# Two neighbouring nodes in one partition: 512-byte rows of x and of the output, and every second column of adj read by TensorE

## The reference

```
h = relu(layernorm(x)); e = par * (diag * h @ W) + h        # W, par, diag of users / of items
x = x + layernorm(adj @ (adj.T @ e)) * gamma + beta + h     # layer 0: adj and its transpose
h = relu(layernorm(x)); x = x + adj @ h                     # layer 1
h = relu(layernorm(x)); x = x + chebyshev(adj, h) + bias    # layer 2: three products with adj
h = relu(layernorm(x))                                      # layer 3
x = x + relu(d * ((adj + I) @ (d * (h @ W3 + b)))), d = degree ** -0.5
```

## Time and profile before

| | us |
|---|---|
| median of 3 runs | 1507.28 (1506.65 to 1507.91) |
| the profiled execution | 1505.76 |
| its span in the trace | 1503.9 |
| TensorE busy (matmul) in it | 1468.5 (98%) |
| VectorE / ScalarE / GpSimd busy | 377.2 / 256.9 / 84.4 |
| mean DMA rate | 354 GB/s |
| granted TensorE clock, mean | 0.997 of 2.4 GHz |

### The profile page before, as it was taken

How to read it: one execution, slowest core, us unless ns; L and a number is a source line. 1 busy time by engine, 2 the same in 40 slices (tenths; PEclk the granted TensorE clock), 3 DMA queues, 4 the chain that set the end, 5 groups by cost and what they waited for, 6 DMA issues and landing times.

```text
span 1503.9 us, 17963 instructions
## 1 busy us (share of the span) xinstructions
PE 1468.5 (98%) x7901; PEld 628.6 (42%) x7901; DVE 377.2 (25%) x383; ACT 256.9 (17%) x510; POOL 84.4 (6%) x67
## 2 busy tenths in 40 slices
PE   6999999999999998999999999999999999999996
PEld 4555555555555653333333333333333333333331
DVE  5683543443443424110110200000000011110210
ACT  3334334344344352000000000000000000000000
POOL 2300000000000017200000000000000000000000
PEclk9999999999999999999999999999999999999999
DMA  9899999999999999999998777979797845598997
GB/s 325 337 415 414 400 392 389 387 386 399 377 396 361 358 396 423 420 421 421 420 420 316 297 280 294 411 292 356 291 319 269 305 172 226 233 398 336 394 420 303
DMA packets 103217, 532.66 MB, mean 354 GB/s; under 512 B 19388, under 2 KB 19428, under 8 KB 55268
## 3 DMA queue, kind: packets, MB, share of 16 engines
q1 hardware_dynamic: 96052, 529.84, 89.8%
q10 hardware_dynamic: 7088, 1.67, 0.5%
HBM read 425.32 MB, written 106.17 MB: 353 GB/s over the span
## 4 chain that ended last, share of the span: by engine, by line
PE 92%; DMA 6%; DVE 1%; POOL 1%; ACT 0%; issue 0%; ACTq 0%; POOLq 0%; DVEq 0%
PE acc L466 34%; PE turned L466 31%; PE turned L492 12%; PE t_acc L477 12%; DMA over_last<-adj_t 6%; PE t_acc L607 1%; DMA w_in<-in_L_gnn_W_i_dram 0%; PE turned L633 0%; PE turned L639 0%; PE acc L518 0%; PE t_rows L617 0%; PE t_acc L542 0%; POOL rstd L982 0%; PE t_rows L531 0%; ACT staged L677 0%
## 5 line engine op out<-in xcount | busy, mean ns | idle before, releaser
L677 ACT ACTIVATE staged<-turned 128x512 f32<-128x512 f32 x400 | 204.2, 615 | 268.5 <-PE turned L492 268.0
L810 DVE TENSOR_REDUCE deg_part<-raw 128x4 f32<-128x3072 f32 (+1 forms) x70 | 220.1, 3192 | 0.0
L492 PE MATMUL turned<-ident,raw 128*128 128x128 f32 x1600 | 190.7, 275 | 0.0
L492 PEld LDWEIGHTS turned<-ident,raw 128*128 128x128 f32 x1600 | 173.8, 140 | 40.3 <-issue 38.7
L466 PE MATMUL acc<-staged,t_cur 128*64 128x512 f32 x800 | 186.9, 601 | 1.6 <-ACT t_cur L714 1.5
L477 PE MATMUL t_acc<-raw,E 128*64 128x384 f32 (+1 forms) x1120 | 184.2, 473 | 0.0
L466 PE MATMUL turned<-over_last,C 128*64 128x512 f32 x680 | 153.5, 593 | 0.0
L466 PE MATMUL turned<-over_last,R 128*64 128x512 f32 x568 | 130.8, 595 | 4.8 <-DMA over_last<-adj_t 4.8
L477 PEld LDWEIGHTS t_acc<-raw,E 128*64 128x64 f32 x1120 | 79.7, 138 | 103.9 <-issue 97.9
L982 POOL TENSOR_TENSOR rstd<-rstd,minus_half 128x8 f32<-128x8 f32 (+1 forms) x30 | 43.8, 1461 | 1300.6 <-DVE rstd L801 1300.6
L466 PE MATMUL acc<-over_last,R 128*64 128x512 f32 x504 | 114.5, 596 | 0.4 <-DMA over_last<-adj_t 0.4
(11 more groups left out here) (125 smaller groups left out, 760.7 us busy)
## 6 DMA issues: line engine op xcount, KB each, us to landing
over_last<-adj_t SPq DMA_DIRECT2D x203, 1024.0 KB, 12.1
raw<-in_adj_dram SPq DMA_DIRECT2D x60, 1536.0 KB, 16.1
adj_t<-staged SPq DMA_DIRECT2D x60, 1536.0 KB, 13.3
staged<-adj_t SPq DMA_DIRECT2D x80, 1024.0 KB, 11.0
over_wide<-adj_t SPq DMA_DIRECT2D x21, 1024.0 KB, 10.8
raw<-in_adj_dram SPq DMA_DIRECT2D x10, 1024.0 KB, 11.3
adj_t<-staged SPq DMA_DIRECT2D x10, 1024.0 KB, 9.8
out_dram<-sq ACTq DMA_DIRECT2D x5, 256.0 KB, 30.2
```

The costliest lines, as they stand in the source:

```text
L492: last = nc.tensor.transpose(turned[q % TURN_BANKS][:, a * P:(a + 1) * P], raw_of(g, u // 2 * 2 + b)[:, sub, c * P:(c + 1) * P], ident[:, :])
L677: nc.scalar.activation(staged_of(g, u)[:, i * B:(i + 1) * B], turned[q % TURN_BANKS][:, :], ACT.Copy) \
L810: nc.vector.tensor_reduce(deg_part[:, of(m), g], raw_of(g, m), AX.X, ALU.add).then_inc(deg_summed, 1)
```

## The change

Before, node t * 128 + p lay in partition p. After, nodes 2p and 2p + 1 of each block of 256 lie in partition p. A row of x, of the output and of diag then comes in pairs: a packet moves two neighbouring rows, 512 bytes, and x and the output have half as many packets. Rows of adj in a partition change with it, and a load of a block of adj becomes two DMAs, one for each 256 rows, with the pieces as before (3072 bytes). The columns of adj have to be taken in the same order, so the transposes read every second column of raw (every_second), and the products of adj.T take even columns for h = 0 and odd ones for h = 1. The copy from t_rows to t_cur becomes a plain one, and diag is turned by two transposes of 20 x 128.

```
-        adj_v = adj_d.rearrange("(m a p) k -> p m a k", a=SUB, p=P)
-        x_v = x_d.rearrange("(t p) d -> p t d", p=P)
-        out_v = out_d.rearrange("(m a p) d -> p m a d", a=CH, p=P)
+        adj_v = adj_d.rearrange("(m b p e) k -> p m b e k", b=SUB // 2, e=2, p=P)
+        x_v = x_d.rearrange("(b p e) d -> p b (e d)", p=P, e=2)
+        out_v = out_d.rearrange("(m b p e) d -> p m b (e d)", b=CH // 2, e=2, p=P)
...
+        def every_second(v, b, e):
+
+            return v[:, 2 * b * P:2 * (b + 1) * P].rearrange("p (k e) -> p e k", e=2)[:, e, :]
...
             def load_first(m):
-                sp.dma_start(raw[:, m], adj_v[:, m, :, 0:GW]).then_inc(raw_in[m], 16)
+                for b in range(SUB // 2):
+                    sp.dma_start(raw[:, m, 2 * b:2 * b + 2, :], adj_v[:, m, b, :, 0:GW]).then_inc(raw_in[m], 16)
...
-                src = adj_v[:, m, :, (g + 1) * GW:(g + 1) * GW + chunks(g + 1) * P]
-                sp.dma_start(raw_of(g + 1, m), src).then_inc(raw_in[m], 16)
+                for b in range(SUB // 2):
+                    src = adj_v[:, m, b, :, (g + 1) * GW:(g + 1) * GW + chunks(g + 1) * P]
+                    sp.dma_start(raw_of(g + 1, m)[:, 2 * b:2 * b + 2, :], src).then_inc(raw_in[m], 16)
...
-                pe.wait_ge(raw_in[m], g * 16 + 16)
+                pe.wait_ge(raw_in[m], 32 * (g + 1))
                 columns = chunks(g) * P // 2
                 for a in range(SUB):
                     for h in range(2):
                         last = nc.tensor.matmul(t_acc[h * D:(h + 1) * D, 0:columns], E[:, m * SUB + a, :],
-                                                raw_of(g, m)[:, a, h * columns:(h + 1) * columns],
+                                                raw_of(g, m)[:, a, :].rearrange("p (k e) -> p e k", e=2)[:, h, :],
...
                         last = nc.tensor.transpose(turned[q % TURN_BANKS][:, a * P:(a + 1) * P],
-                                                   raw_of(g, u // 2 * 2 + b)[:, sub, c * P:(c + 1) * P], ident[:, :])
+                                                   every_second(raw_of(g, u // 2 * 2 + b)[:, sub, :], c // 2, c % 2), ident[:, :])
...
-            nc.tensor.transpose(t_rows[:, 0:NT], diag_rows, ident[0:NT, 0:NT]).then_inc(diag_turned, 1)
+            for e in range(2):
+                last = nc.tensor.transpose(t_rows[:, e * NT // 2:(e + 1) * NT // 2], every_second(diag_rows, 0, e),
+                                           ident[0:NT // 2, 0:NT // 2])
+            last.then_inc(diag_turned, 1)
...
-                act.dma_start(out_v[:, m], out_rows[m % 2][:, :, :]).then_inc(out_stored[m % 2], 16)
+                act.dma_start(out_v[:, m], out_rows[m % 2][:, :, :].rearrange("p (b e) d -> p b (e d)", e=2)).then_inc(out_stored[m % 2], 16)
```

More of the change, by code:

```diff
@@ L207, in gnn_stack @@
         S = [cen[1][:, i * SUB:(i + 1) * SUB, :] for i in range(2)]
-        diag_rows = t_t[0:NT, 0:P]
+        diag_rows = t_t[0:NT // 2, 0:2 * P]
         over_last = [sb(f"over_last{j}", [P, TILE_WORDS]) for j in range(NB)]
@@ L394, in load_x @@
             def load_x(i):
-                t = slice(X_PARTS[i][0] * SUB, X_PARTS[i][1] * SUB)
-                sp.dma_start(X[:, t, :], x_v[:, t, :]).then_inc(x_in[i], 16)
+                first, last = X_PARTS[i]
+                sp.dma_start(X[:, first * SUB:last * SUB, :].rearrange("p (b e) d -> p b (e d)", e=2),
+                             x_v[:, first * SUB // 2:last * SUB // 2, :]).then_inc(x_in[i], 16)
             def load_first(m):
-                sp.dma_start(raw[:, m], adj_v[:, m, :, 0:GW]).then_inc(raw_in[m], 16)
+                for b in range(SUB // 2):
+                    sp.dma_start(raw[:, m, 2 * b:2 * b + 2, :], adj_v[:, m, b, :, 0:GW]).then_inc(raw_in[m], 16)
             load_x(0)
-            sp.dma_start(diag_rows[0:U // P, :], du_d.rearrange("(t p) -> t p", p=P)).then_inc(diag_in, 16)
-            sp.dma_start(diag_rows[U // P:NT, :], di_d.rearrange("(t p) -> t p", p=P)).then_inc(diag_in, 16)
+            sp.dma_start(diag_rows[0:U // (2 * P), :], du_d.rearrange("(b n) -> b n", n=2 * P)).then_inc(diag_in, 16)
+            sp.dma_start(diag_rows[U // (2 * P):NT // 2, :], di_d.rearrange("(b n) -> b n", n=2 * P)).then_inc(diag_in, 16)
             load_x(1)
@@ L686, in _ @@
             act.wait_ge(diag_turned, 1)
-            nc.scalar.activation(diag[:, :], t_rows[:, 0:NT], ACT.Copy).then_inc(diag_ready, 1)
+            nc.scalar.activation(diag[:, :].rearrange("p (b e) -> p e b", e=2),
+                                 t_rows[:, 0:NT].rearrange("p (e b) -> p e b", e=2), ACT.Copy).then_inc(diag_ready, 1)
             for m in range(NB + 2):
@@ L713, in take_t @@
                 half = chunks(g) // 2
-                nc.scalar.activation(t_cur[:, 0:2 * half, :].rearrange("p (h b) d -> p b h d", h=2),
-                                     t_rows[:, 0:half * P].rearrange("p (b h d) -> p b h d", b=half, h=2), ACT.Copy) \
-                    .then_inc(t_ready, 1)
+                nc.scalar.activation(t_cur[:, 0:2 * half, :], t_rows[:, 0:half * P].rearrange("p (c d) -> p c d", d=D),
+                                     ACT.Copy).then_inc(t_ready, 1)
             def end_of_layer(v):
@@ L807, in sum_rows @@
             def sum_rows(g, m):
-                dve.wait_ge(raw_in[m], g * 16 + 16)
+                dve.wait_ge(raw_in[m], 32 * (g + 1))
                 nc.vector.tensor_reduce(deg_part[:, of(m), g], raw_of(g, m), AX.X, ALU.add).then_inc(deg_summed, 1)
```

## The result

The changed kernel takes 1532.39 us (median of 4 runs, 1531.35 to 1533.25) against 1507.17 for the kernel before on the same chip: a ratio of 1.0167, 95% interval 1.0152 to 1.0182, slower by 25 us. The forecast was 1505.1 us in a range of 1502.5 to 1515. The profiled execution has a span of 1531.4 us, 27.5 more than before.

A forecast was written before the change was run, and what follows sets the result against it. TensorE was taken to hold 92% of the chain, with DMA leading near the end. Terms 0 + 0 - 0.9 - 1.0 - 0.3 = -2.2 us, taken off the median 1507.28, gave 1505.1 us, range 1502.5 to 1515.

The forecast's parts named there:

- The strided reads: Stage one: TensorE reading every second value of raw costs 0, with bounds 0 and +351 us.
- rival C: Stage one: TensorE reads every second value more slowly; 1676 or 1856 us if fully, 1509 to 1524 if partly; 17%.
- mild form: Stage one: strided reads only partly slower, 1 to 5% of 375 us, +4 to +19, so 1509 to 1524; 8%.
- The doubled loads: Loads of adj: 140 DMAs instead of 70 are hidden and cost 0, with bounds 0 and +2 us.
- rival D: Loads of adj: two DMAs cost more than one, +1.1 us x 70 = +77, giving 1584 us; 4%.
- The start: Before TensorE's first product: fewer packets of x bring w_in sooner, -0.9 us, with bounds 0 and -1.5.
- Rival B: Start and stores: w_in held by its own latency, 512-byte packets costing twice 256-byte ones, no gain, 1507.3 us; 14%.
- The output stores: Stretch DMA holds at the end: four stores in half as many packets save 1.0 us, bounds 0 and -2.1.
- with bytes alone, 0: Bound for stores among the last loads: if their cost goes with bytes alone, larger packets gain 0.
- The last store: Very end, nothing beside it: 32 packets an engine instead of 64, -0.3 us, with bounds 0 and -0.5.

The follow-up runs named there:

- products_second_apart: Kernel before, with the products of adj.T reading every second column and the two halves taking different rows a: 1516.84 us, ratio 1.0069.
- split_loads: Kernel before, with each load of a block of adj as two DMAs of half the size and nothing else: 1505.82 us, ratio 0.9994.
- x_out_pairs: Kernel before, with x loaded and the output stored in packets of 512 bytes and nothing else: 1506.23 us, ratio 0.9999.
- both_plain: Changed kernel, with transposes and products both reading neighbouring columns of raw again: 1505.34 us, ratio 0.9995 to the kernel before.

## Why the prediction was wrong

**The strided reads** were the step that failed. I put them at 0, and they cost 29.5 us of busy time and 25 to 27 us of run time. The bounds, 0 and +351, held it, and rival C named the slower reads and their place and that they decide from 0.6%; but its mild form was sized at 1 to 5% of 375 us, up to +19, and it was 7.9%. By its parts: weight loads from 107 to 120 ns apart, 12.6 ns x 1600 = 20 us, and products from 161 to 169 ns, 8 ns x 1120 = 9 us. The reasoning for 0 was that 2 cycles per value leave the reader room to throw half of the neighbours away. The moving operand shows what is wrong with it: with half of them used it already costs 5%, with a quarter 110%. By the estimate above the reader brings two values in 1.76 ns where it had 1.68: the room was almost enough and not enough. For the stationary operand, two thirds of the loss, the runs show the price (12.6 ns a load, for a step of two and of four) and that the step is its cause, but not what in the load takes the time. A term of 375 us deserved more than an argument with ends at 0 and 100%: 0.6 per cent of it was as much as everything else in the sum.

The reason given in C for the mild form (both halves fetch the same neighbours) was wrong, as products_second_apart shows. The other half of that reason, that VectorE sums the block and DMA writes the next at the same time, was not tried alone, but the trace speaks against it: in the changed kernel the last load into raw is issued at 547 us and has landed by 559, and VectorE's last sum of rows ends at 565. A run of 16 weight loads behind that still takes 1.99 to 2.00 us; in the same stretch of the kernel before it is 1.73 to 1.78 (timelines, before and then changed):

```profile
560.69 1.73 PEld L492 LDWEIGHTS turned<-ident,raw 128*128 128x128 f32 x16 [0.81 <-ACT staged L677]
```

```profile
572.68 1.99 PEld L499 LDWEIGHTS turned<-ident,raw 128*128 128x128 f32 x16 [0.81 <-issue]
```

DMA was just as busy there with other tiles, so a part of it in the price isn't ruled out.

**The doubled loads** were right: hidden, and rival D fell (0.9994 in split_loads). SyncE's issue grew by more than the 0.37 us I counted, since a load of half the size issues in 0.61 us in the median in the changed kernel, 1.2 us for a pair; between 60 and 520 us TensorE has no wait for raw at all.

**The start** (-0.9) did not come: the moment went from 10.58 to 11.57 us, and in the means of the traces from 11.1 to 11.5, under a scatter of 1 us. I took the making of packets as what w_in waits for, from half-empty DMA slices and the 2.08 us in which SyncE issues the last part of x. That issue does shrink, to 0.71 us, and w_in is no earlier; from 3.3 to 5 us the slices are no fuller with half the packets of x, 0 to 5 tenths in the changed kernel and 0 to 6 in x_out_pairs. Rival B had this right; its other half, a 512-byte packet at twice the price of one of 256, is wrong, as the stores show. What w_in does wait for stays open.

**The output stores** (-1.0): the price of a packet was right, 27.5 ns forecast and 26.5 measured, and with it the share of the queue, 5.0% for 4.7. That this moves the last tile was wrong. In 26 us the tile loads moved 10.53 MB before and 10.54 after, though the stores beside them took less time. Both queues together moved 10.89 and 10.93 MB: in this stretch the DMA engines move some 420 GB/s either way, and the time that a store packet takes is not taken from the loads' bytes. That was the bound "with bytes alone, 0". **The last store** (-0.3) was right, 2.6 to 2.3 us; it is the only gain that the traces show, and too small to be seen in the time.

So even without the strided reads the forecast should have been about 1507 and not 1505.1, the time of case B: both_plain is 1.2 us under the kernel before, in an interval that holds 0, and x_out_pairs 0.5.

## What to carry to other kernels

A step in what TensorE reads has to be priced against the whole time of the operand, not against what the new layout saves: here 8% on two groups of matmuls made 2% of all of TensorE's time, and the packets it bought were worth some 0.3 us in the trace and nothing in the measured time. If a layout needs a step somewhere, put it into a small operand or one whose load is hidden (the 64 columns of E cost nothing), and don't let the moving operand use fewer than two of four neighbouring values: one of four doubled its time. And where a single early trace gives a moment that a microsecond hangs on, take its scatter from other traces before it becomes a term.

## What the runs showed of the hardware that was not expected

- Moving fp32 operand, two halves side by side: 161 ns for a record of 384 columns with four values used of each 16 bytes, 169 with two (adjacent or not), 338 with one.
- Stationary fp32 operand of 128 columns, loads back to back: 107 ns apart with neighbouring columns, 120 with every second and with every fourth alike, and 140, 209 and 210 ns long. The price does not grow from a step of two to one of four. With 64 columns, a step of two and room between loads, a load is 2 ns longer.
- Store packets of 256 and 512 bytes among 8 KB loads take 17.8 and 26.5 ns, yet the loads beside them move the same bytes in the same time.
